# A graph-attention kernel: edge loops in rounds of 16 chunks and a ring of four quads, against 24 and six

## The reference

```python
x = x + L0_gnn(layernorm(x))     # weighted sum over the edges
x = x + L0_ffn(layernorm(x))     # one small attention over 32768 edges picks 2 of 4 experts
x = x + L1_gnn(layernorm(x))     # three attention layers over the 50000 edges
x = x + L1_ffn(layernorm(x))     # 8 experts, 2 used
```

```python
e = leaky_relu(e_src[src] + e_dst[dst], 0.2)
ex = exp(e - segment_max(e, dst)[dst])
out = segment_sum(h[src] * (ex / segment_sum(ex, dst)[dst])[:, :, None], dst)
```

## Time and profile before

| | us |
|---|---|
| median of 3 runs | 4251.59 (4249.4 to 4253.91) |
| the profiled execution | 4245.6 |
| its span, first to last instruction | 4243.7 |
| gate attention, first to last gather | 1200.8 to 1559.2 |
| layer 1, first to last gather | 2018.7 to 2587.8 |
| layer 2, first gather of it | 2688.01 |
| layer 3, first gather of it | 3348.11 |

### The profile page before, as it was taken

How to read it: one execution, slowest core, us unless ns; L and a number is a source line. 1 busy time by engine, 2 the same in 40 slices (tenths; PEclk the granted TensorE clock), 3 DMA queues, 4 the chain that set the end, 5 groups by cost and what they waited for, 6 DMA issues and landing times. The chain is left out here.

```text
span 4243.7 us, 90071 instructions
## 1 busy us (share of the span) xinstructions
PE 2972.7 (70%) x23551; PEld 1861.0 (44%) x23551; DVE 2901.4 (68%) x9716; ACT 2273.2 (54%) x7990; POOL 2415.7 (57%) x2564
## 2 busy tenths in 40 slices
PE   5589937666666649997577666577766677766188
PEld 4352213333343337775344444344443444444166
DVE  6779957777547772224687777588777588777715
ACT  2008913333257762112687774488776387777423
POOL 4777767777357750000777774577775477777010
PEclk8679979999655559998555556655555755555599
DMA  2000023333221110001644443544444544444000
GB/s 97 6 2 2 2 74 105 105 106 105 49 14 10 10 30 12 12 0 39 137 108 108 108 108 65 123 108 109 108 108 86 112 109 108 108 108 102 3 23 30
DMA packets 200139, 292.98 MB, mean 69 GB/s; under 512 B 110595, under 2 KB 140254, under 8 KB 199934
## 3 DMA queue, kind: packets, MB, share of 16 engines
q0 software_dynamic: 108656, 245.98, 23.2%
q1 hardware_dynamic: 91310, 44.97, 4.4%
HBM read 270.29 MB, written 20.50 MB: 69 GB/s over the span
## 5 line engine op out<-in xcount | busy, mean ns | idle before, releaser
L889 POOL DMA_INDIRECT work<-table_att,work x1368 | 1294.2, 946 | 919.6 <-ACT work L990 503.1
L1061 PE MATMUL psum<-ident,work 128*128 128x128 f32 x1656 | 558.5, 474 | 357.1 <-ACT work L1014 357.1
L1014 ACT ACTIVATE work<-work 128x128 f32<-128x128 f32 x1656 | 529.3, 390 | 235.5 <-DVE work L929 235.5
L1069 PE MATMUL psum<-work 128*32 128x65 f32 (+1 forms) x13248 | 418.7, 295 | 314.0 <-ACT work L1021 272.6
L1061 PEld LDWEIGHTS psum<-ident,work 128*128 128x128 f32 x1656 | 301.4, 182 | 657.6 <-ACT work L1014 487.0
L1069 PEld LDWEIGHTS psum<-work 128*32 128x32 f32 x13248 | 330.8, 165 | 433.7 <-DVE acc L923 372.7
L929 DVE SCALAR_TENSOR_TENSOR work<-psum,work 128x128 f32<-128x128 f32 x1656 | 464.8, 343 | 79.3 <-ACT work L1004 75.7
L923 DVE SCALAR_TENSOR_TENSOR acc<-acc,work,psum 128x65 f32 (+1 forms) x1656 | 445.1, 269 | 81.4 <-DMA acc<-table_att 15.3
L1004 ACT ACTIVATE work<-psum,work 128x128 f32<-128x128 f32 x1656 | 475.1, 375 | 46.0 <-DVE work L939 44.5
L471 POOL DMA_INDIRECT sorted<-xt x400 | 392.5, 981 | 169.6 <-issue 121.3
L1053 PE MATMUL psum<-ident,work 128*128 128x128 f32 x1656 | 461.9, 435 | 36.5 <-DVE work L908 35.5
(11 more groups left out here) (310 smaller groups left out, 4562.7 us busy)
## 6 DMA issues: line engine op xcount, KB each, us to landing
work<-table_att,work POOLq DMA_INDIRECT x1368
table_att<-acc SPq DMA_DIRECT2D x75, 132.0 KB
acc<-table_att SPq DMA_DIRECT2D x12, 812.5 KB
work<-table_sum,index POOLq DMA_INDIRECT x415, 2.7
sorted<-xt POOLq DMA_INDIRECT x400, 2.1
work<-table_gate,work POOLq DMA_INDIRECT x288, 2.4
work<-in_L_ffn_W_dram SPq DMA_DIRECT2D x8, 512.0 KB, 5.0
table_sum<-acc SPq DMA_DIRECT2D x25, 128.0 KB
```

The lines of the kernel that those rows point to most:

```text
L889: nc.gpsimd.indirect_dma_start(out=rows[s][:, t, :], out_offset=None, in_=table[:, 0:rw], in_offset=bass.IndirectOffsetOnAxis(ap=f.index[s ...
L1014: nc.scalar.activation(f.pt[s % 2][:, t, :], f.y[s % 2][:, t, :], ACT.Exp, bias=f.neg[s][:, t, 1:2]).then_inc(exped, 1)
L1061: nc.tensor.transpose(ps_p[s % 2][:, t * P:(t + 1) * P], f.pt[s % 2][:, t, :], m.ident[:, :]).then_inc(turned2, 1)
L1069: ins = nc.tensor.matmul(ps_s[s % 2][DB * h:DB * (h + 1), t, :], f.p[s % 2][:, t, DB * h:DB * (h + 1)], rows[s][:, t, h * w1:(h + 1) * w1] ...
```

## The change

One constant:

```diff
--- before.py
+++ after.py
@@ -18,7 +18,7 @@
 GN = 5
 HEADS = 4
 QD = 4
-GROUP = 24
+GROUP = 16
 DB = 32
```

## The result

The changed kernel takes **4319.65 us** (median of 4 runs, 4317.8 to 4324.19), the kernel before beside it 4251.55 us (4 runs, 4249.4 to 4253.91). The ratio is 1.0161 with an interval of 1.0148 to 1.0173: 68 us slower. The forecast was 42.5 us slower, 4294 us, with a range of 4260 to 4325. The sign was right, and 26 us were missing from the sum.

What follows compares the result with a forecast made beforehand. The prediction took POOL's back-to-back gather issue, allowed by the ring of six, as the bound. Its terms, -30 + 44 + 20.5 + 14 - 6 = +42.5 us on 4251.6, gave 4294 us, range 4260 to 4325.

Steps and rivals of the forecast that it cites:

- two quads fewer: Each layer has 112 quads instead of 114, saving 10.0 us of POOL a layer, 30.0 us in three.
- loop of waits: Mid-layer, POOL to landing, mask, PE and back: 15.44 us for three quads against POOL's 15.01; 44 us lost in three layers.
- start of a layer: With four slots, quad 6 waits for quad 2, held by the own rows' load; 20.5 us lost in three layers.
- late landings: In a layer's last third every third quad lands late; each excess is paid in full, 14 us lost.
- end of a layer: The last gathers start 0.83 us after PE ends quad 107, giving back 2.0 us a layer, 6 us.
- the gate: Its loop takes 14.4 us, under 15.0, so POOL stays the limit: no change, at most 1 us.
- The main case: The summed terms, 4294 us, with allowances a span of 4275 to 4313 us; chance 0.63.
- loop turns that refetch: Rival: 33 more turns in layers and gate fetch instructions again at 0.5 us each, 16 us, 4310 us; chance 0.05.
- a POOL that wakes slower: Rival: a waiting POOL needs 1.1 us or more after PE, loop 15.7 or more, 28 us on top, 4322 us; chance 0.08.
- What bounds the kernel: In layers and gate POOL issues gathers back to back, 5.00 us a quad, because six slots let it run ahead of PE.
- The rival in which the ring just suffices: In the layers the loop is 15.0 us or less and POOL stays the limit: -14, 4238 us; chance 0.08.
- POOL issues without a stop: Layer 1's 455 idle gaps, none over 0.3 us, were read as never a real wait, giving 5.00 us a quad.

Runs made afterwards that it cites:

- the spread padding's run: Changed kernel with padding entries of the gather lists sent to row 24 times the partition instead of row 0: 4305.55 us beside 4249.93.
- the undisturbed kernel: The changed kernel with the gather lists' padding entries pointing at different rows, read between POOL's pauses: 4305.55 us, ratio 1.0134 to the kernel before.
- the wait for five back: Kernel before, POOL waiting for the quad five back instead of six: 4266.03 us beside 4250.75; 5474.17 beside 5490.05 and 5429.08 beside 5446.18.
- the rounds of 32: Rounds of 32 chunks with eight slots, against the kernel before's 24 and six: 5474.36 us beside 5490.05, 5432.29 beside 5446.18, 5432.08 beside 5444.9.

## Why the prediction was right, and where it was short

Its terms against what they measured, in three layers and the gate:

| term | forecast | measured | from |
|---|---|---|---|
| two quads fewer | -30 | -30 | 2 x 5.00 x 3, counted |
| loop of waits | +44 | +46 | 102 x (5.152 - 5.003) x 3 |
| start of a layer | +20.5 | +25.2 | quad 0 to quad 9 |
| late landings | +14 | +14 | the spread padding's run |
| end of a layer | -6 | -10 | last quad's first gather to PE's end: 19.9 / 20.0 / 20.0 for 23.1 / 23.0 / 23.8 |
| pauses in the layers | 0 | +19 | 12 x 1.6, an estimate |
| the gate | 0 | +4.4 | 3.0 of it two pauses |
| sum | +42.5 | +68.6 | 71.2 in the stages' own spans, 68.1 between the medians |

The main case had been given 4275 to 4313 us, and 4319.65 lies outside of it. The stated range holds the time only because it had been drawn wider, for loop turns that refetch and for a POOL that wakes slower, and neither is what happened. That the time lies in the range is in part luck.

**What bounds the kernel** was read rightly: POOL's uninterrupted issue, held up by the room in the ring. The rival in which the ring just suffices needed 0.4 us from PE to POOL; it is 0.81 at the least. The Trainium skill's figure on its side (DMA: Bandwidth & Descriptors, section Anatomy of one DMA — SWDGE (gpsimd) path; by it an estimate of 2.31 us for a landing) stays below what the trace after shows again: 2.85 us from the gather to the mask, and a median of 2.77 to the last landing signal on record. The rival of a POOL that wakes slower named about the right time (4322) for a wrong reason.

**The loop of waits** is the best of the terms: 15.46 measured in the undisturbed kernel for 15.44 worked out from four rows. The loop turns cost nothing that shows, and no instruction packets fall into the loops (17470 packets of the gathers' queue alone, as in the earlier trace rows). The rule of Runtime: NRT & Kernel Launch, section Instruction fetch mechanics, of the Trainium skill speaks of a branch out of the fetched window. That short bodies don't meet it is what the trace has; the eight-quad bodies do fetch inside their loops, 58 packets on one instruction queue from 2720 to 3350 where the wait for five back beside it has 2, and at a pace of 6.6 us a quad that can't be priced.

**The step that failed** is the one that says "POOL issues without a stop", taken from gaps "none over 0.3 us". It is true of the gathers and not of POOL's sequencer, which stops for 2.35 us every 96 gathers, and the gathers run on because it is ahead. The forecast let the ring take away the lead over PE and kept, unasked, the lead that hid this. These pauses are +19 in the layers and 3.0 of the gate's +4.4, so 22 of the missing 26 us. In the gate they are most of the error of "at most 1 us": there the loop of waits is short enough, as forecast, but the lead is 1.42 us instead of 11.3, and two gaps grow by 1.45 and 1.53.

**The start of a layer** was 4.7 us short in one term. The forecast let the own rows land 2.5 us sooner because 5 gathers fall out of that stretch; they land 0.7 and 2.9 us sooner and 0.9 later, 0.9 on the mean. The queues from 2028 to 2061 answer to the earlier trace rows:

```profile
q1 hardware_dynamic: 13674, 3.43, 72.5%
q0 software_dynamic: 992, 2.83, 40.2%
```

The gathers' share fell from 45.2 to 40.2% as thought, but the same 13674 packets of the load took 72.5% instead of 64.5, so here little was freed for it. That need not be the rule. In the kernel before that waits for four back, where POOL is held in the same way, PE ends quad 2 2.0, 2.8 and 1.7 us sooner than before, and the three starts cost 20.3 us, the forecast's 20.5. The load's end differs by 1 to 3 us from trace to trace, and one trace of each kernel can't tell this term's error from that.

**The end of a layer** gave back 1.3 us more a layer than forecast: PE takes 2639.89 - 2619.19 = 20.7 us for the last four quads, where the 21.9 of the earlier trace rows was assumed.

**What was to show it**: first to last gather 594.5 us, not 584; POOL's idle time beyond its gaps of 0.3 in layer 1 is 594.5 - 447 x 1.251 = 35 us, and 29 without the pauses, inside the 25 to 30 named; it names PE far less often than was said, since a wait that PE has just ended is booked as issue.

## What to carry to other kernels

When a ring's room shrinks, write down the loop of waits over all the engines that a slot passes through and compare it with the pace of the bounding engine times the quads in flight: that gave the steady loss to 5%, and it is a threshold and not a slope (in the middle of a layer, six and five slots 0, four slots 5 us in 100). Then ask what else the lead was hiding. An engine that "never waits" in the rows may be covering a stop of its own sequencer, a slow load at the start or a late landing. Each of them was harmless here while the lead lasted, and reached the time once it was gone.

And where a row names no one for a wait ("remote", "issue"), ask which semaphore the sequencer passed and when the signal was due. Here that turned a pause of POOL into a late signal of PE.

## What the runs showed of the hardware that was not expected

- POOL's sequencer takes 1.91 us to issue four indirect gathers of 128 rows, and every 96 (in the changed kernel 104, in the rounds of 32 88) gathers 4.1 to 4.5 us. From PE's end to the start of a gather on a waiting POOL it takes 0.81 to 0.84 us in half of the cases, of which 0.75 lie behind the passed wait.
- Gathers with many indices on row 0 land up to 1 us later (3.88 against 2.82 us from gather to mask).
- In the sittings where the kernel before takes 5445 to 5490 us, PE's signal of a finished quad reaches the others a median of 4.1 to 4.7 us after the last matmul instead of 0.04. The landings are not late: the last landing signal on record comes a median of 2.77 us after the fourth gather's start, as before.
- There, waiting for the quad four back made rounds of 32 46 to 53 us faster (5432.29 to 5385.94; 5474.36 to 5421.78). Without that wait the mask of a quad follows its fourth gather after 25.8 us (median of layer 1), since DVE is that far behind, with it after 2.9; PE ends the last quad 37.5 us after its first gather instead of 20.1, and layer 1 takes 764.8 us to PE's end instead of 757.6. The pace is 6.62 and 6.67 us a quad in the two, so running ahead gained nothing there and cost the longer end.
